# Sliding-window attention in double steps: scores of two query tiles at once, a fixed accumulator for each projection unit, and another load order in the opening

## The reference, cut to what matters

```
q, k, v = x @ Wq, x @ Wk, x @ Wv                 # 32 heads of 64
scores = q . k / 8 + bias(head, distance)        # each 512-block sees itself and the block before
scores = where(0 <= distance < 512, scores, -1e30)
m = max(scores.max(-1), sink)
p = exp(scores - m);  denom = p.sum(-1) + exp(sink - m)
out = (p @ v) / denom @ Wo
x = layernorm(x + out)
```

## Time and profile before

| | |
|---|---|
| median of 3 runs | 916.93 us (916.65 to 919.36) |
| the profiled execution | 914.45 us, span of its slowest core 912.9 us |
| spans of the cores | 908.0 to 912.9 us, granted TensorE clock 0.978 to 0.981 |
| TensorE busy | 849.6 us of the span |
| VectorE, ScalarE busy | 494.7 and 425.7 us |

### The profile page before, as it was taken

How to read it: one execution, slowest core, us unless ns; L and a number is a source line. 1 busy time by engine, 2 the same in 40 slices (tenths; PEclk the granted TensorE clock), 3 DMA queues, 4 the chain that set the end, 5 groups by cost and what they waited for, 6 DMA issues and landing times.

```text
span 912.9 us, 18322 instructions; the slowest of 8 cores (908.0 to 912.9 us)
## 1 busy us (share of the span) xinstructions
PE 849.6 (93%) x5880; PEld 466.0 (51%) x5880; DVE 494.7 (54%) x1511; ACT 425.7 (47%) x928; POOL 149.1 (16%) x285
## 2 busy tenths in 40 slices
PE   2499999999999999999999999999599999889996
PEld 0154665555556546556556555554244545444442
DVE  2016756556566565565665655656466437535644
ACT  2026666666666666666666666665200512221000
POOL 6211304301111030030130110026100000000000
PEclk9799999999999999999999999999799999999999
DMA  8999698996795898998988869649949473001312
GB/s 125 149 170 165 89 120 105 166 170 84 99 152 71 124 129 93 130 117 100 113 118 129 114 110 128 131 52 161 201 98 224 86 125 70 1 1 68 155 55 92
DMA packets 127820, 104.73 MB, mean 115 GB/s; under 512 B 81328, under 2 KB 114096, under 8 KB 126192
## 3 DMA queue, kind: packets, MB, share of 16 engines
q0 software_dynamic: 40032, 53.53, 40.7%
q1 hardware_dynamic: 87696, 50.04, 33.6%
HBM read 125.91 MB, written 8.59 MB: 147 GB/s over the span
## 4 chain that ended last, share of the span: by engine, by line
PE 88%; DMA 6%; POOL 2%; issue 1%; ACT 1%; DVE 1%; DVEq 0%; ACTq 0%; POOLq 0%
PE psP L385 18%; PE psP L356 17%; PE psP L369 12%; PE psS L629 7%; PE psT L469 6%; PE psP L629 5%; PE psP L516 5%; PE psS L516 5%; PE psS L405 5%; PE psP L496 4%; DMA sb<-wv 3%; DMA sb<-xr 2%; POOL sb L200 1%; DMA sb<-wo 1%; PE psT L576 1%
## 5 line engine op out<-in xcount | busy, mean ns | idle before, releaser
L428 DVE CUSTOM_DVE_ANT_0 sb<-psS,sb 128x641 f32<-128x641 f32 (+4 forms) x256 | 171.5, 689 | 116.5 <-PE psS L405 98.0
L445 ACT ACTIVATE sb<-sb 128x641 bf16<-128x641 f32 x256 | 211.9, 833 | 32.0 <-DVE sb L428 16.0
L356 PE MATMUL psP<-sb 128*128 128x512 bf16 x768 | 180.7, 382 | 20.9 <-DMA sb<-xt 20.7
L385 PE MATMUL psP<-sb 128*128 128x256 bf16 x1536 | 180.6, 275 | 10.9 <-DMA sb<-wv 10.7
L485 ACT ACTIVATE sb<-psT 128x640 bf16<-128x640 bf16 x128 | 90.0, 703 | 195.9 <-PE psT L469 195.9
L385 PEld LDWEIGHTS psP<-sb 128*128 128x128 bf16 x1536 | 149.0, 99 | 31.9 <-issue 14.2
L421 DVE CUSTOM_DVE_ANT_0 sb<-psS,sb 128x512 f32<-128x512 f32 (+3 forms) x128 | 62.7, 490 | 129.1 <-PE psS L405 127.3
L356 PEld LDWEIGHTS psP<-sb 128*128 128x128 bf16 x768 | 71.5, 98 | 99.2 <-issue 25.1
L369 PE MATMUL psP<-sb 128*128 128x512 bf16 x512 | 119.4, 383 | 0.0
L457 DVE TENSOR_SCALAR sb<-sb 128x640 bf16<-128x640 bf16 x256 | 88.0, 386 | 13.8
L369 PEld LDWEIGHTS psP<-sb 128*128 128x128 bf16 x512 | 48.6, 99 | 52.2 <-issue 1.4
(11 more groups left out here) (102 smaller groups left out, 699.5 us busy)
## 6 DMA issues: line engine op xcount, KB each, us to landing
sb<-gscr SPq DMA_DIRECT2D x32, 320.0 KB, 11.0
sb<-wk POOLq DMA_DIRECT2D x64, 128.0 KB, 12.6
sb<-wv POOLq DMA_DIRECT2D x64, 128.0 KB, 9.6
sb<-wq POOLq DMA_DIRECT2D x64, 128.0 KB, 15.4
sb<-gscr SPq DMA_DIRECT2D x32, 256.0 KB, 13.5
sb<-wo POOLq DMA_DIRECT2D x64, 128.0 KB, 14.3
sb<-wt POOLq DMA_DIRECT2D x4, 2048.0 KB, 16.5
y<-sb SPq DMA_DIRECT2D x16, 512.0 KB, 3.0
```

Of the source, the lines that this page charges most:

```text
L356: tok = put("T", lambda t, i=i: t.matmul(bank_ap(bank, [1, 512]), b(WK[pr % 2] + i * 128, [1, 128]), b(XT[blk] + i * 512, [1, 512]), start ...
L385: tok = put("T", lambda t, i=i: t.matmul(bank_ap(bank, [1, 256]), b(XT[blk] + i * 512 + part * 128, [1, 128]), b(WV[g % 2] + i * 256, [1, ...
L428: ttr_last[pr] = ttr_tok[u, hh] = put("V", lambda v: v.tensor_tensor_reduce(out=f(sx + 2 * halo, [1, 641 - halo]), in0=p(psS[hh], 192 + ha ...
L445: e_tok[u, hh] = put("S", lambda s: s.activation(b(pslot(u, hh), [1, 641]), f(SX[hh], [1, 641]), ACT.Exp, bias=f(st + 4 * hh + 2, [1, 1]), ...
```

## The change

Steps are taken two at a time (a *double step* m, tiles u and u + 1; a pair has four, m = 0 to 3, of which 0 and 1 have n = 0). Its parts:

- `scores(u)` puts the scores of both tiles of both heads into `psS0` and `psS1`, now three banks each (bank numbers 1 to 3 and 4 to 6): 8 matmuls of 384, 256, 256 and 384 columns instead of twice 4 of 320.
- All four `bias_min` and `exponent` stand ahead of the projections in the queues of VectorE and ScalarE, tile by tile.
- `psP` is one bank (number 0). Each double step runs two whole units: the first into bank 0, the second into bank 6, the last third of `psS1`, which also holds the end of the scores of head 1 of tile u + 1. The transposes and `pv` stand inside and behind the second unit. `pv` writes into `psT`'s bank.
- The sink no longer stands as a 641st column of the bias; it is the starting value of the first minimum of a tile, read from memory where a constant stood.
- V is projected two tiles to a bank, with one copy of 512 columns.
- Opening: K of pairs 0 and 1 and the first four V tiles run in turn by quarters of x; the loads go in that order, and weights of the opening come in larger pieces.

```diff
+    banks = [(psP, 0)] + [(psS[i // 3], 512 * (i % 3)) for i in range(6)]
...
+        free = [bank_free[k] for k in range(1, 7)]
+        after = [k_tok[pr, n], k_tok[pr, n + 1], q_tok[pr, n]]
+        for which, base, c0, w in ((0, T0, 0, 384), (0, T0, 384, 256),
+                                   (1, T1, 0, 256), (1, T1, 256, 384)):
...
+                bank = 3 * hh + (base + c0) // 512
...
+                    after=after + [free[bank]], mark=(which == 1))
...
-            after=[s_tok[u, hh], bias_tok[pr, hh], sink_tok[pr, hh], first,
-                   e_tok.get((u - 1, hh))], mark=True)
+            after=[s_tok[u, hh], bias_tok[pr, hh], first, t_neg, e_tok.get((u - 1, hh))],
+            mark=True)
+        ttr_last[pr] = ttr_tok[u, hh] = tok
+        for k in ((1, 2) if c % 2 else (0,)):
+            bank_free[1 + 3 * hh + k] = tok
...
         scores(u)
-        if u > 1:
-            transpose(u - 2, 0)
-            unload(u - 2, 0)
-        bias_min(u, 0)
-        bias_min(u, 1)
-        feed.run(quota * 0.25)
-        exponent(u, 0)
-        feed.run(quota * 0.2)
...
+        for w in (u, u + 1):
+            for hh in range(2):
+                bias_min(w, hh)
+                exponent(w, hh)
+        normalise(u)
+        normalise(u + 1)
...
+        feed.begin(0)
+        feed.run()
+        feed.begin(6)
+        turns = [(w, hh) for w in (u, u + 1) for hh in range(2) if not by_dma(w, hh)]
+        share = {2: (0.45, 0.35, 0.2), 4: (0.2, 0.25, 0.25, 0.2, 0.1)}[len(turns)]
+        if c == 2:
+            pending_pv.append((m + (2 if by_dma(u, 1) else 1), pr, n))
+        late_turn = None
+        for w, hh in turns:
+            feed.run(8192 * share[turns.index((w, hh))])
+            if (w, hh) == turns[-1] and not (pending_pv and m >= pending_pv[0][0]):
+                feed.run()
+            transpose(w, hh)
+            unload(w, hh)
+        feed.run()
+        pv_due(m)
```

Opening loads (POOL's queue):

```diff
-    load_wk(0)
+    load_wk(0, 2048)
+    load_x(0, (0,))
...
-    load_wk(1)
-    load_x(0)
-    load_wv(0)
-    load_wq(0)
+    load_wk(1, 2048)
+    load_wv0(0)
+    for q in range(1, 4):
+        load_x(0, (q,))
+        load_wv0(q)
+    load_wq(0, 2048)
```

More of the change, by code:

```diff
@@ L87, in __init__, with add, begin, run @@
         self.work = collections.deque()
[L88 to L108, removed]
+        self.live = None
+    def add(self, unit):
+        self.work.append(unit)
+    def begin(self, bank=None):
+        self.live = self.work.popleft()(bank) if self.work else None
+    def run(self, cols=None):
+        while self.live is not None and (cols is None or cols > 0):
+            done = next(self.live, None)
+            if done is None:
+                self.live = None
+            elif cols is not None:
+                cols -= done
     def drain(self):
         while self.work:
-            self.one()
-        self.debt = 0.0
+            self.begin()
+            self.run()
 def build_program(nc):
@@ L207, in build_program, with pieces, load_wk, load_wq @@
     x_tok = [[None] * 4 for _ in range(3)]
[L209 to L215, removed]
+    def pieces(dst, src, row0, cols, width, after):
+        toks = []
+        for j in range(0, 2048, width):
+            toks += [load_cast(dst + j, src, row0, cols, width, after=after, c0=j)] * (width // 512)
+        return toks
+    def load_wk(pr, width=512):
+        wk_tok[pr] = pieces(WK[pr % 2], wk_in, pr * 128, NI * 128, width, [wk_done.get(pr - 2)])
+    def load_wq(pr, width=512):
+        wq_tok[pr] = pieces(WQ[pr % 2], wq_in, pr * 128, NI * 128, width, [wq_done.get(pr - 2)])
     def load_wv(g):
@@ L310, in build_program @@
         after=[t_gh], dma=True) for k in range(2)]
-    t_pz = [vop(lambda v, k=k: v.memset(p(psS[k], 192 + 640, [1, 1]), 0.0)) for k in range(2)]
     bias_tok, halo_tok = {}, {}
@@ L346, in bank_ap, with k_group @@
     def bank_ap(bank, *dims, rows=128):
-        tens, off = bank if isinstance(bank, tuple) else (bank, 0)
-        return p(tens, off, *dims, rows=rows)
+        return p(bank[0], bank[1], *dims, rows=rows)
     k_tok, q_tok, v_tok = {}, {}, {}
     s_last, pv_last = {}, {}
-    def k_group(pr, blk):
-        k, bank = next_bank()
+    def k_group(pr, blk, k=None):
+        k, bank = next_bank(k)
         for i in range(NI):
@@ L443, in exponent @@
     def exponent(u, hh):
+        pr, n, c = steps[u]
         st = STA[u % 4]
+        if n == 0 and c == 0:
+            sink_tok[hh] = put("S", lambda s: s.activation(
+                f(SX[hh] + 2 * 640, [1, 1]), f(NSK + 2 * (2 * pr + hh), [1, 1]), ACT.Copy),
+                after=[t_neg, e_tok.get((u - 1, hh))], mark=True)
         e_tok[u, hh] = put("S", lambda s: s.activation(
@@ L597, in router @@
         rs = RTS[t % 2]
-        tens, off = bank if isinstance(bank, tuple) else (bank, 0)
+        tens, off = bank
         lg, mx, rep, mr, ex, wd = (f(rs + 16 * j, [1, 8]) for j in range(6))
@@ L810, in build_program @@
         t_rep[k] = vop(lambda v, k=k: v.memset(f(RTS[k] + 32, [1, 8]), HUGE), *late)
-    for i in range(4):
-        banks.append((psS[i // 2], 512 * (i % 2)))
-        release(3 + i, ttr_tok[U, i // 2])
     feed.drain()
```

230 lines of the change are left out of this document (120 added, 110 removed).

## The result

The changed kernel is slower: the ratio of the times is **1.083**, with an interval of 1.080 to 1.086. The profiled execution took 993.4 us, where I had written 986. (Some executions of the changed kernel, up to 1068.8 us, two of the three of the variant const_init and one of loads_small were lengthened by a lower clock on one die, and no time of theirs is compared with anything here.)

What follows compares the result with a forecast made beforehand. TensorE bounds the kernel, so its waits add in full: +61 us (pairs 1 to 14), +8 (pair 0), +2 (pair 15), -1 (opening) make +70 on the median 916.93: 987, written 986; 8 in 10 for 957 to 1008.

Steps and rivals of the forecast that it cites:

- Which engine and where: Steady part, from pair 3 on: TensorE is always busy, so any wait given to it adds to the time in full.
- The wait for bank 6: Second unit's first matmul waits for the last of four minima: 1.72, 1.64, 0.50 and 0.36 us in a pair's double steps.
- The wait at `pv`: `pv` writes `psT` and waits for ScalarE's copy of the last transposes: 0.58 and 0.47 us, once each per pair.
- 0.93 saved at the brackets: TensorE's loss around scores: 64 brackets for 128 save 0.75 us per pair, `pv` directly before scores 0.18.
- Pairs 1 to 14: Fourteen steady pairs: 5.27 us of waits less 0.93 gives +4.34 per pair, +61 us in all.
- Pair 0: First pair, both heads transposed through the single `psT`: waits, four bare turns and 1.7 us for a clock fall; +8 us.
- Pair 15 and the end: Longer double steps fill the existing 9.33 us wait for residual rows, what follows is about as long; +2, between -3 and +8.
- Opening: Up to the first scores: same bytes awaited, fewer issues on POOL; -1 us, bounds -6 to +3.
- Rival 1: Only halo steps (n = 0) wait; waits of n = 1 and `pv` vanish, 27 us less: 959; 15 in 100.
- Rival 3: Bank 6 is free in time, at 0.79 us or less per minimum; only bracket savings remain: 904 us; 5 in 100.
- Rival 2: TensorE's clock also falls after the waits in 28 halo double steps: 48 us more, 1034; 11 in 100.
- Rival 4: The opening decides: -6 us there gives 981, which can't turn the sign; no separate chance given.

Runs made afterwards that it cites:

- const_init: Changed kernel with a constant as the starting value of a tile's first minimum, the sink left out of the maximum; 984.7 us, pairs of 40.26.
- loads_small: Kernel before the change with the change's order of opening loads, in the old pieces of 512 columns; median 914.4 us, ratio 0.9994.
- bank3: Changed kernel with the second unit in bank 3 instead of bank 6; 953.1 us, pairs of 37.90.
- early_turns: Changed kernel with its two turns of transposes after 5 and 10 of the second unit's 16 matmuls instead of 8 and 14; 982.4 us, pairs of 40.00.
- alternate2: The kernel of alternate with the first turn of transposes after 10 instead of 12 matmuls of the second unit; 943.4 us, undisturbed pairs of 36.62.
- bank4: Changed kernel with the second unit in bank 4 instead of bank 6; 968.4 us, pairs of 38.77.
- loads_only: Kernel before the change with the change's order of opening loads and its larger pieces; median 923.3 us, ratio 1.0062.
- alternate: Changed kernel, tiles swapping places in psS each double step, `pv` between the units, first unit's copy behind the first transposes; median 957.1 us, ratio 1.040.

## Why the prediction was right, point by point

- **Which engine and where**: right. Pairs 1 to 14 were TensorE's alone, and every wait came out in the time. const_init shows it closest: 0.06 us per minimum on another engine, 0.7 per pair.
- **The wait for bank 6**, 4.22 per pair: right in place, and in size partly by luck. From start to start it is 1.77 in m = 0 (1.72 predicted), 1.38 in m = 1 (1.64), 0.61 in m = 2 (0.50) and 0.28 in m = 3 (0.36). Together 4.04. Shown by bank3, which changes nothing but the bank. In m = 0 the bank is free at 5.89 for 5.87, because two errors cancel: the first minimum starts 0.14 earlier than worked out, and "Exponents don't lengthen this chain" is wrong by 0.17. In m = 1 and 3 TensorE comes to the bank 0.2 later than at the 4.15 of the prediction, held by the copy of the second unit.
- **The wait at `pv`**, 1.05: right. The rows of 0.51 and 0.40, with the 0.16 and less 0.09 for the bracket, are 0.58 and 0.47; early_turns took 0.95 away.
- **0.93 saved at the brackets**: not tried by itself. The waits of 4.04 and 1.05 and twice the 0.22 of the copy, less 0.93, make 4.60, and 4.47 was measured, so it is near; the pair of 36.62 in alternate2 fits the 0.75 of it that are scores. ScalarE's copy holds the last score in m = 1 and 3 by 0.2 as forecast, "only where the wait for bank 6 takes it up"; it mattered in alternate2, where no such wait is left.
- **Pairs 1 to 14**: 4.47 per undisturbed pair, 62.6 for fourteen; the rest of the 63.8 is 0.7 for pairs that last up to 41.2 and not 40.95, and 0.5 from the kernel before, whose pair 1 lasts 35.73. Against +61.
- **Pair 0**: +7.05 for +8, with the four bare turns where I put them. I had counted 1.7 for a fall of the clock that didn't come (1.00 in the row of this stretch, 0.95 before), so the waits themselves are 0.3 to 0.7 longer than worked out, by the unrounded sum or by +8. Over the cores pair 0 lasts 43.9 to 44.6 after; before it lasts 36.8 on two cores and 35.2 on the other six, so on most cores the difference is near 9.
- **Pair 15 and the end**: mis-sized, +6.0 for +2, within the -3 to +8 that I gave it. The step "longer double steps in pair 15 fill a hole that is there anyway" was right: the hole went from 9.33 to 3.78. What failed is "what stands behind it ... is about as long". The last `pv` starts 62.8 us after the pair's first score, and before the corresponding one starts at 60.4: +2.5, with the waits of 3.78, 2.79 and twice 0.94 at the transposes in it. After it another 3.5 are lost. By the weight loads 402 Wo matmuls stand behind the last `pv` for 395 before: 7 of 0.216, 1.5 us. The other 2.0 of this core lie behind the attention: VectorE's last instruction ends 7.0 us before the end of the span (984.32 to 991.3), and before 4.9 (907.97 to 912.9); this is the store of the result. On six of the eight cores after it takes 4.9 to 5.0 as before, only on 4 and 5 the longer time.
- **Opening**: -1 was wrong in sign, but over the cores the first scores are at 64.2 to 65.0 after and 62.5 to 65.4 before. So it is about nothing, 0.2 in the mean. In the profiled core 0.84 of it is a wait right before the first scores, for ScalarE's copies of the last units (64.98, 0.84 <- ACT L480).
- **Rival 1** (only the halo steps wait) fell with the waits of 0.45 and 0.51. **Rival 3** fell: 1.17 to 1.30 from one minimum to the next is far from 0.79. **Rival 2** (the clock) fell: the granted clock of pairs 1 to 14 is 1.00, with 28 waits of 1.4 to 1.8 in them. By the Trainium skill, "TensorE: Matmul & The Clock Gate", section "A second HAM failure mode: psum-queue depth-cycling", this pattern of small gaps from cycling through PSUM banks is one that makes the clock go up and down; the trace of this kernel doesn't agree for its gaps. **Rival 4** (the opening) moved the time by 1.5 us, inside its bounds.

## What to carry to other kernels

When a buffer is cut for two tiles at once, ask of each piece who reads it last and who wants it first, and don't give the first writer the piece whose last reader comes last: one bank number was worth 40 of the 77 us here. The piece that is free earliest needn't be the best either: bank4 gave 15 of the 40 back, since the next scores want this bank first and the operands behind it weren't ready. If the readers go through a temporary that exists once, the engine that empties it belongs to the chain. When two short steps are merged into one long one on the engine that is the bound, the dependent chain on the engines beside it doubles and its cover doesn't; compare chain and cover before counting the overhead saved. And test a change's loads apart from the rest: these made nothing faster in the opening and cost the kernel before 0.6%, most of it in a stretch 100 us later.

## What I had not expected of the hardware

- Larger pieces of load brought no speed at all at this place, with eight cores loading at once. The Trainium skill ("DMA: Bandwidth & Descriptors", section "Bandwidth") advises batches of 1 MiB or more for three quarters of the peak, and says that its figures are of one core alone; the pieces here were 256 and 512 KB in place of 128 KB, so its size isn't reached. The run with the larger pieces had its first scores no earlier, and its core 0 moved 144 GB/s in the first 62 us, for 151 with the small ones.
- DMA transposes came late enough for TensorE to wait 3 to 6 us for one (3.85 in loads_only, up to 6.3 in alternate), on some of the cores and not on others. That the loads beside them are the reason is argued from loads_only and loads_small, not tried step by step.
- Single waits of 1.4 to 1.8 us, one in each of 28 double steps of some 10 us with full groups on both sides, didn't lower TensorE's granted clock.
